# Alignment: the step comparisons on GpSimd as difference and sign, the step choice twelve rows behind, its edge moved before the sums' edge

## The reference, cut to what matters

```python
def _dtw_cost(D):
    row0 = jnp.cumsum(D[0])
    def row_step(prev_row, d_row):
        first = d_row[0] + prev_row[0]
        def col_step(left, inp):
            d_ij, up, diag = inp
            r = d_ij + jnp.minimum(jnp.minimum(up, left), diag)
            return (r, r)
        ...
def _backtrack(R, T1, T2):
    ...
        cd = jnp.where((i > 0) & (j > 0), R[jnp.maximum(i - 1, 0), jnp.maximum(j - 1, 0)], BIG)
        cu = jnp.where(i > 0, R[jnp.maximum(i - 1, 0), j], BIG)
        cl = jnp.where(j > 0, R[i, jnp.maximum(j - 1, 0)], BIG)
        choice = jnp.argmin(jnp.stack([cd, cu, cl]))
```

## Time and profile before

| | |
|---|---|
| median of 3 runs | 4342.56 us (4341.47 to 4342.78) |
| the profiled execution: span, first to last instruction | 4342.4 us; no time around it is shown apart |
| the loop of the alignment, in the profiled execution | 135.7 to 313.6 us |
| VectorE busy in the whole span | 3360.0 us (77%) |
| GpSimd busy in the whole span | 1017.5 us (23%) |
| TensorE's mean granted clock, whole span | 0.921 of 2.4 GHz |

### The profile page before, as it was taken

One profiled execution on the slowest core, in us unless ns is written; L12 is line 12 of the kernel. 1 busy time (PEld: TensorE's weight loads), 2 busy tenths in 40 slices (PEclk: granted clock), 3 DMA queues, 4 the chain that ended last, 5 costly groups with the idle time before them and its releaser, 6 DMA issues. The chain is left out here.

```text
span 4342.4 us, 70861 instructions
## 1 busy us (share of the span) xinstructions
PE 3490.1 (80%) x25855; PEld 2819.6 (65%) x25855; DVE 3360.0 (77%) x5326; ACT 2818.1 (65%) x4654; POOL 1017.5 (23%) x929
## 2 busy tenths in 40 slices
PE   6445749999999788999999975777777777777787
PEld 3334337999999566899999852555555555555676
DVE  4675877777777633877778656999999999999744
ACT  3112616666666443666666542999999999999932
POOL 0000503111220201121112010434444444444310
PEclk9555869999999888999999987999999999999998
DMA  8743011111110021111111001000000000000000
GB/s 270 114 59 109 4 41 39 39 31 39 34 37 16 23 66 36 31 39 31 31 39 31 9 20 41 16 16 16 16 31 16 16 16 18 29 16 8 1 23 18
DMA packets 186341, 161.29 MB, mean 37 GB/s; under 512 B 7996, under 2 KB 174092, under 8 KB 185996
## 3 DMA queue, kind: packets, MB, share of 16 engines
q1 hardware_dynamic: 182604, 142.83, 12.5%
q10 hardware_dynamic: 3392, 13.93, 0.9%
HBM read 127.36 MB, written 20.20 MB: 34 GB/s over the span
## 5 line engine op out<-in xcount | busy, mean ns | idle before, releaser
L559 PEld LDWEIGHTS psU<-ctxN,ST 128*128 128x128 f32 x6656 | 853.7, 191 | 98.4 <-issue 39.7
L559 PE MATMUL psU<-ctxN,ST 128*128 128x129 f32 x6656 | 868.1, 275 | 20.7 <-issue 20.7
L1174 DVE MAX8 top<-pairs 128x8 f32<-128x801 f32 (+1 forms) x512 | 702.8, 1398 | 0.1
L1136 POOL TENSOR_TENSOR P<-P,EX 128x1601 f32<-128x1601 f32 x128 | 460.4, 3597 | 705.8 <-ACT P L1051 705.8
L645 ACT ACTIVATE ST<-ST 128x512 f32<-128x512 f32 (+1 forms) x832 | 513.2, 625 | 167.1 <-DVE ST L747 163.1
L945 PE MATMUL psU<-ctxN,PT 128*128 128x129 f32 (+1 forms) x3328 | 429.9, 280 | 200.6 <-ACT PT L1059 200.6
L747 DVE TENSOR_TENSOR ST<-ST,psB 128x512 f32<-128x512 f32 (+1 forms) x832 | 556.2, 677 | 3.4 <-PE psB L578 3.4
L733 DVE TENSOR_TENSOR psA<-psA,ST 128x512 f32<-128x512 f32 x640 | 446.6, 698 | 137.4 <-ACT ST L637 69.4
L945 PEld LDWEIGHTS psU<-ctxN,PT 128*128 128x128 f32 (+1 forms) x3328 | 393.0, 192 | 224.8 <-ACT PT L1059 224.7
L1184 DVE MATCH_REPLACE8 pairs<-top,pairs 128x801 f32<-128x801 f32 (+1 forms) x384 | 480.1, 1255 | 0.0
L547 PE MATMUL psS<-statL,ctxH 128*128 128x512 f32 x832 | 393.6, 473 | 5.7 <-ACT ST L637 2.7
(11 more groups left out here) (505 smaller groups left out, 6216.5 us busy)
## 6 DMA issues: line engine op xcount, KB each, us to landing
ctxN<-in_ctx SPq DMA_DIRECT2D x48, 768.0 KB
ahead_ctxT<-ctxT_scratch SPq DMA_DIRECT2D x32, 800.5 KB, 4.4
ctxT_scratch<-trn ACTq DMA_DIRECT2D x16, 800.5 KB
ctxT<-ctxT_scratch SPq DMA_DIRECT2D x16, 800.5 KB, 6.1
nat<-in_ctx SPq DMA_DIRECT2D x16, 768.0 KB
dist_scratch<-dd SPq DMA_DIRECT2D x8, 800.5 KB
skewed<-in_ctx SPq DMA_DIRECT2D x8, 768.0 KB
ctx_late<-in_ctx SPq DMA_DIRECT2D x8, 768.0 KB
```

The costliest lines, as they stand in the source:

```text
L559: last = pe.matmul(psU[:, q, 0:D + 1], ST[0:n, i % SLOTS, q * 128:q * 128 + 128], ctxN[0:n, j, k, 0:D + 1], start=(k == 0 and q % 2 == 0), ...
L1136: pool.tensor_tensor(P[:, j, :], P[:, j, :], EX[:, j, :], ALU.mult).then_inc(p_ready, 1)
L1174: dve.max(top_t[:, 8 * n:8 * n + 8], pairs_t[:, 0:HALF if n < 2 else KP]).then_inc(listed_early if n < 2 else listed_late, 1)
```

## The change

GpSimd takes over `find_stays` and `find_slants`, each as two instructions: a difference, and its comparison with zero in place (is_lt; is_le, times 0.75). Four instructions of 804 elements per batch are added on GpSimd, 72 in all, with a wait for its own result between the two of a pair. `find_moves` stays on VectorE as one `tensor_tensor` with a maximum, since the factor 0.75 is already in `slant`. `LAG` grows from 8 to 12 rows, `m`, `stay` and `moves` go from two buffers to three, `slant` from one to two. On TensorE and ScalarE the drift's step now stands before the sums' step. Two semaphores are added.

```diff
-    LAG = 2 * G
+    LAG = 3 * G
+    KEPT = 3
...
+                    def find_stays(k):
+                        w, at = rows_of(k), ring(k * G)
+                        cell = stay[:, k % KEPT, 0:w, 1:ROWS + 1]
+                        pool.wait_ge(scanned, k * G + w + ONE)
+                        if k >= KEPT:
+                            pool.wait_ge(drifted, (k - KEPT + 1) * G + ONE)
+                        pool.tensor_tensor(cell, rows[:, at + 1:at + w + 1, 0:ROWS], m[:, k % KEPT, 0:w, 1:ROWS + 1],
+                                           ALU.subtract).then_inc(stay_parted, 1)
+                        pool.wait_ge(stay_parted, k + 1 + ONE)
+                        pool.tensor_scalar(cell, cell, 0.0, None, ALU.is_lt).then_inc(stay_ready, 1)
+
+                    def find_slants(k):
+                        w, at = rows_of(k), ring(k * G)
+                        cell = slant[:, k % 2, 0:w, 1:ROWS + 1]
+                        if k >= 2:
+                            pool.wait_ge(moves_ready, k - 1 + ONE)
+                        pool.tensor_tensor(cell, rows[:, at:at + w, 0:ROWS], rows[:, at:at + w, 1:ROWS + 1],
+                                           ALU.subtract).then_inc(slant_parted, 1)
+                        pool.wait_ge(slant_parted, k + 1 + ONE)
+                        pool.tensor_scalar(cell, cell, 0.0, DIAGONAL, ALU.is_le, ALU.mult).then_inc(slant_ready, 1)
+
+                    for k in range(NB):
+                        find_stays(k)
+                        find_slants(k)
...
                     for s in range(STEPS + LAG):
+                        if s - LAG >= 1:
+                            move_drift(s - LAG)
                         if s < STEPS:
                             if s == RING:
                                 pe.wait_ge(row_carried, 1 + ONE)
                             move_cost(s)
-                        if s - LAG >= 1:
-                            move_drift(s - LAG)
...
-                        if s >= 2 * G:
-                            act.wait_ge(stay_ready, s // G - 1 + ONE)
+                        if s >= KEPT * G:
+                            act.wait_ge(stay_ready, s // G - KEPT + 1 + ONE)
...
                     for s in range(STEPS + LAG):
+                        if s >= LAG:
+                            set_drift_edge(s - LAG)
                         if s < STEPS:
                             if s == RING:
                                 carry_row()
                             set_edge(s)
-                        if s >= LAG:
-                            set_drift_edge(s - LAG)
...
+                    def find_moves(k):
+                        w = rows_of(k)
+                        dve.wait_ge(stay_ready, k + 1 + ONE)
+                        dve.wait_ge(slant_ready, k + 1 + ONE)
+                        if k >= KEPT:
+                            dve.wait_ge(drifted, (k - KEPT + 1) * G + ONE)
+                        dve.tensor_tensor(moves[:, k % KEPT, 0:w, 1:ROWS + 1], slant[:, k % 2, 0:w, 1:ROWS + 1],
+                                          stay[:, k % KEPT, 0:w, 1:ROWS + 1], ALU.max).then_inc(moves_ready, 1)
+
                     for s in range(NB * G + LAG):
                         if s < STEPS:
                             nearer(s)
-                        k, part = s // G - 1, s % G
-                        if 0 <= k < NB:
-                            if part == 0:
-                                find_stays(k)
-                            elif part == 1:
-                                find_slants(k)
-                            elif part == 2:
-                                find_moves(k)
+                        if s >= LAG - 1 and s % G == G - 1 and s // G - KEPT + 1 < NB:
+                            find_moves(s // G - KEPT + 1)
                         if 0 <= s - LAG < STEPS:
                             scan_drift(s - LAG)
                         if s < STEPS:
```

More of the change, by code:

```diff
@@ L3350, in align @@
             rows = c.sb(s2, "rows", [128, RING + 1, ROWS + 1])
[L3351 to L3354, removed]
+            m = c.sb(s2, "m", [128, KEPT, G, ROWS + 1])
+            stay = c.sb(s2, "stay", [128, KEPT, G, ROWS + 1])
+            slant = c.sb(s2, "slant", [128, 2, G, ROWS + 1])
+            moves = c.sb(s2, "moves", [128, KEPT, G, ROWS + 1])
             next_block = c.sb(s2, "next_block", [128, 128])
@@ L3363, in align @@
             stay_ready, slant_ready, moves_ready = c.sem("stay_ready"), c.sem("slant_ready"), c.sem("moves_ready")
+            stay_parted, slant_parted = c.sem("stay_parted"), c.sem("slant_parted")
             drifted, drift_moved, drift_edge = c.sem("drifted"), c.sem("drift_moved"), c.sem("drift_edge")
@@ L3398, in align, with rows_of, batch, ring @@
             with nc.Block() as block:
+                def rows_of(k):
+                    return min(G, STEPS - k * G)
+                def batch(s):
+                    return s // G % KEPT, s % G
+                def ring(s):
+                    return s % RING
                 @block.gpsimd
@@ L3500, in nearer @@
                             dve.wait_ge(row_carried, 1 + ONE)
-                        if s >= 2 * G:
-                            dve.wait_ge(stay_ready, s // G - 1 + ONE)
+                        if s >= KEPT * G:
+                            dve.wait_ge(stay_ready, s // G - KEPT + 1 + ONE)
                         dve.tensor_tensor(m[:, j, n, 1:ROWS + 1], rows[:, ring(s), 0:ROWS],
@@ L3513, in scan_cost @@
                                                ALU.min, ALU.add).then_inc(scanned, 1)
[L3515 to L3536, removed]
                     def scan_drift(s):
```

## The result

| | before | with the change |
|---|---|---|
| median of the runs | 4342.02 us | 4368.95 us (4367.03 to 4370.78) |
| span of the profiled execution | 4342.4 us | 4366.4 us |
| cost scan of row 3 to the end of the last drift scan | 167.9 us | 193.8 us |
| four rows (cost scan of row 40 to that of row 44) | 9.44 us | 10.62 us |

The change makes the kernel slower: ratio 1.0057, 95% interval 1.0045 to 1.0069, +26.9 us. The loop of the alignment accounts for it: +25.9 us from row 3 to the last drift scan. The loop's head and the 6.1 us behind the loop are the same. The two profiled executions as a whole are only 24.0 us apart, so the rest of the kernel differs by some 2 us the other way.

The account below looks back on a forecast made before the run. It took the alignment loop as bound equally by vector work and the order of the two edges. Rows 12 to 70 +25, early rows +0.5, tail +9 and clearing semaphores +0.3 made +35 us: 4378 us, range 4350 to 4430.

Parts of the forecast that it names:

- Exclusion: Alignment loop: two-SBUF-input VectorE instructions, scans included, and GpSimd's SBUF reads run strictly in turn; 4.44 us per batch.
- Rival 1: Alignment loop: the engines do not exclude each other; -31 us, 4312 us, faster; chance 0.14.
- rival 2: Alignment loop: only `nearer` and the choice collide with GpSimd, scans do not; +12 us, 4355; chance 0.10.
- The sum per batch: Four rows of the loop: vector work, exclusion and a remaining edge wait, 11.12 us against 9.42 before.
- The comparison: GpSimd's comparison with zero on 804 elements: 0.87 us each, 2.35 as the upper end.
- rival 3: Alignment loop: all collide and GpSimd's comparison is dear; +87 us, 4430; chance 0.20 including prices between it and the forecast.
- The edge order: TensorE and ScalarE queues: with the drift's edge first, the one row in four without wide work falls from 2.35 us.
- The floor that the sum builds on: Four loop rows if GpSimd cost nothing: three at 1.62 us, one at 2.35, 7.21 us in all.
- The early rows and the tail: Rows 1 to 11: +0.5 us. After the last cost scan: four more drift scans and GpSimd's share, +9 us.

Follow-up runs that it names:

- pool_no_read: The change with GpSimd's four instructions per batch replaced by fills of the same tiles, same waits and signals; median 30.0 us below before, four rows 7.13 us.
- pool_elsewhere: The change with GpSimd's four instructions on a tile of their own that VectorE never touches; median 19.4 us above before, four rows 10.38 us.
- moves_in_psum: The change with `moves` in PSUM (two buffers), so the drift scan reads one SBUF and one PSUM tensor; median 5.6 us above before, ratio 1.0015.
- order_only: The kernel before with only the drift's edge moved ahead of the cost's on TensorE and ScalarE; median 20.3 us below before, four rows 8.41 us.
- order_lag12: order_only with the drift twelve rows behind and three buffers, nothing on GpSimd; median 7.3 us below before, ratio 0.9983, four rows 8.42 us.

## Why the prediction was right

Direction, mechanism and range held: +26.9 us against +35 forecast, with 4350 to 4430 as the range. By its own steps:

- **Exclusion.** The step that decided, taken from one pair of rows in another stage, holds for the scans as well: pool_no_read removes it, pool_elsewhere shows that it is not the data, moves_in_psum that the drift scan is out of it with one of its two operands in PSUM. The rule drawn on from the Trainium skill (SBUF — State Buffer, section Who interferes with whom) holds as to which instructions collide. For a whole instruction it holds for the differences; a sign lets VectorE through after 0.65 of its 2.4 to 3.0 us, and there the measurement decides. Rival 1 and rival 2 are out.
- **The sum per batch.** Forecast 11.12, measured 10.62: this is the term that was mis-sized, +25 us forecast for rows 12 to 70 against +17.3 from row 11 on. The forecast was 6.43 us of vector work, 4.44 of exclusion and 0.26 of a remaining edge wait. The batch shown above has 6.34, 4.05 and 0.23, which make the 10.62. The vector work is less because the choice counts 0.90 from start to start where its operands are long ready, not 0.99. The exclusion is 0.39 less, and that is the difference of two errors: the path is held for 4.6 us, by the estimate above, where I had 5.52, and only some 0.5 of it is hidden where I had 1.1. Against the batch without reads (7.13) no more than 3.5 us are lost, since that batch has 7.13 - 6.34 = 0.79 us of edge waits, and all but 0.23 of them lie under the exclusion in the change.
- **The comparison.** I took 0.87 us as its duration and kept 2.35 as the upper end. The instruction lasts 2.37 and 3.05 us: the row of 749 ns spoke true and the casts did not. What the Trainium skill says (GPSIMD Engine Reference, section Engine selection), an operation with one input at roughly line rate, does not hold for its duration here. The time was not rival 3's (+87) all the same, because duration was the wrong quantity: it costs VectorE 0.42 us each (0.84 for two). Two errors met here, a wrong duration and the belief that duration is what is paid, and they nearly cancelled: this part of the number is luck. The prediction's own sign of rival 3, both comparisons over 2 us, came true without its time.
- **The edge order.** I took it for worth 0.73 us in one row of four. It was worth 1.03 us in all four, as order_only shows. The floor that the sum builds on was right all the same: the batch without reads takes 7.13 us where I had 7.21, three rows of 1.60 to 1.62 and one of 2.29.
- **The early rows and the tail.** +1.2 against +0.5 and +7.4 against +9; the tail's four scans at 1.46 us were exact (order_lag12, +5.84), GpSimd's share in it is 1.5 us (19.12 against 17.60), where I had 3.

A kernel that beats both exists: order_only, with the comparisons left on VectorE, 0.9959 and 0.9969 of before in two measurements. The order alone gives -15.1 us in the loop; the rest of the change, reads on GpSimd and the longer lag together, costs 41.0 on top of it.

## What to carry to other kernels

Before moving elementwise work from VectorE to GpSimd, look at the operands of what stays behind: where VectorE's instructions read two SBUF tensors, GpSimd's reads held them up here, and an instruction of 0.9 us taken off cost 1.35 for its difference alone (2.70 for two). An operand in PSUM took the drift scan out of this. And where two small transfers share in-order queues, put first the one that is ready first; where a period is the same in rows with and without extra work, suspect that queue in all of them, even where the profile shows no idle time.

## What was not expected of the hardware

- GpSimd's tensor_scalar with a comparison takes 2.37 us (is_lt) and 3.05 us (is_le, then a product) for 804 float32 elements per partition, and yet holds up VectorE for about 0.65 us by the estimate above. That is 0.8 ns per element, near the 0.82 ns per further element of the casts. Why it lets go before its end was not tried.
- A difference takes 1.52 us in the median when both inputs come from `rows`, and 2.05 with `rows` and `m`, of which some 0.3 is waiting for `nearer`. Why the two differ beyond that was not tried.
- GpSimd's fills did not delay VectorE at all: no scan above 0.58 us with 72 fills beside them.
